# A recommender tower on one core: the pair products move to GpSimd, an accumulating DMA folds 12 fields of each tile, and the closing sum comes two tiles later

## The reference, cut to what matters

```python
x0 = prev = e                                     # (512, 32 fields, 32)
for W in (filter_0, filter_1):                    # 32*32 x 128 and 32*128 x 128
    z = einsum('bhd,bmd->bhmd', x0, prev)         # products of pairs
    cur = relu(einsum('bpd,pn->bnd', z.reshape(b, h*m, d), W))
    prev = cur
    outs.append(cur)
h = concatenate([sum over d of outs, dense_ctx])  # 128 + 128 + 16
h = relu(h @ W_top1 + b_top1); h = relu(h @ W_top2 + b_top2); y = h @ W_top3
```

## Time and profile before

| what | us |
| --- | --- |
| median of 3 runs | 1014.85 (1011.53 to 1015.65) |
| the profiled execution, its own time | 1015.16 |
| its span in the trace | 1013.4 |
| DVE busy in it | 962.2 (95%) |
| PE busy | 914.2 (90%) |
| ACT busy | 818.3 (81%) |
| POOL busy | 810.8 (80%) |

### The profile page before, as it was taken

One profiled execution on the slowest core, in us unless ns is written; L12 is line 12 of the kernel. 1 busy time (PEld: TensorE's weight loads), 2 busy tenths in 40 slices (PEclk: granted clock), 3 DMA queues, 4 the chain that ended last, 5 costly groups with the idle time before them and its releaser, 6 DMA issues.

```text
span 1013.4 us, 17901 instructions
## 1 busy us (share of the span) xinstructions
PE 914.2 (90%) x3822; PEld 713.5 (70%) x3822; DVE 962.2 (95%) x1057; ACT 818.3 (81%) x2808; POOL 810.8 (80%) x452
## 2 busy tenths in 40 slices
PE   3989899898999989899999899989899988898998
PEld 2767777777778677677776777767776766677784
DVE  4899999999999999999999999999999999999993
ACT  3878888788888878788888788878888878888892
POOL 5678889788889888889888888888888788896871
PEclk9999999899999989999999899999999999999998
DMA  5412222202222202222211222211222211222000
GB/s 190 133 51 71 71 66 70 59 23 66 71 65 69 69 18 60 70 66 68 69 39 39 70 69 65 70 42 35 71 70 64 69 37 41 70 70 64 1 1 0
DMA packets 42849, 61.18 MB, mean 60 GB/s; under 512 B 6273, under 2 KB 17153, under 8 KB 42786
## 3 DMA queue, kind: packets, MB, share of 16 engines
q1 hardware_dynamic: 38690, 58.48, 18.8%
q0 software_dynamic: 4096, 2.11, 1.4%
HBM read 56.37 MB, written 4.20 MB: 60 GB/s over the span
## 4 chain that ended last, share of the span: by engine, by line
PE 61%; DVE 20%; issue 12%; ACT 3%; POOL 2%; DMA 1%; DVEq 1%; SPq 0%; ACTq 0%; POOLq 0%
PE ps_y L621 17%; PE ps_y L627 17%; PE ps_y L622 16%; DVE csum L514 6%; DVE prod L500 6%; DVE z L474 5%; PE ps_c L608 3%; PE ps_c L609 2%; PE ps_c L610 2%; ACT prod L384 2%; DVE c_lo L479 2%; PE ps_h L632 1%; POOL prod L321 1%; PE ps_c L606 1%; POOL z_lo L310 1%
## 5 line engine op out<-in xcount | busy, mean ns | idle before, releaser
L384 ACT ACTIVATE prod<-ps_y,es 128x128 f32<-128x128 f32 x2560 | 698.8, 416 | 76.2 <-PE ps_y L627 72.6
L321 POOL TENSOR_TENSOR prod<-prod 128x1536 f32<-128x1536 f32 x129 | 450.4, 3491 | 113.6 <-DVE prod L500 96.6
L627 PE MATMUL ps_y<-w_hi,c_lo 128*128 128x512 f32 x1024 | 413.4, 404 | 49.1 <-DVE c_lo L479 49.1
L621 PE MATMUL ps_y<-w_hi,c_hi 128*128 128x512 f32 x1024 | 429.2, 419 | 28.1 <-DVE prod L500 25.0
L622 PE MATMUL ps_y<-w_lo,c_hi 128*128 128x512 f32 x1024 | 411.0, 401 | 0.0
L514 DVE TENSOR_REDUCE csum<-prod 128x64 f32<-128x1280 f32 x256 | 378.2, 1478 | 10.2 <-ACT prod L384 0.6
L474 DVE TENSOR_TENSOR z<-first,second 128x512 f32<-128x512 f32 x160 | 282.1, 1764 | 7.1 <-DMA second<-et_scratch 7.1
L627 PEld LDWEIGHTS ps_y<-w_hi,c_lo 128*128 128x128 f32 x1024 | 198.7, 194 | 105.5 <-DVE c_lo L479 62.0
L500 DVE TENSOR_TENSOR prod<-ps_y,es 128x512 f32<-128x512 f32 x384 | 256.2, 677 | 10.2 <-PE ps_y L627 10.1
L621 PEld LDWEIGHTS ps_y<-w_hi,c_hi 128*128 128x128 f32 x1024 | 198.6, 194 | 94.9 <-DVE prod L500 39.1
L310 POOL TENSOR_TENSOR z_lo<-z,z_hi 128x512 fp32r<-128x512 f32 x155 | 222.3, 1452 | 6.8 <-ACT z_hi L362 6.8
(11 more groups left out here) (59 smaller groups left out, 259.0 us busy)
## 6 DMA issues: line engine op xcount, KB each, us to landing
second<-et_scratch SPq DMA_DIRECT2D x160, 256.0 KB, 4.3
first<-et_scratch SPq DMA_DIRECT2D x32, 256.0 KB, 3.3
et_scratch<-gat SPq DMA_DIRECT2D x64, 64.0 KB
prod<-w SPq DMA_DIRECT2D x4, 512.0 KB, 7.1
gat<-table,rows_now POOLq DMA_INDIRECT x128, 2.4
wt_sb<-wt SPq DMA_DIRECT2D x2, 512.0 KB, 5.5
prod<-w0a SPq DMA_DIRECT2D x1, 320.0 KB, 3.1
prod<-w0b SPq DMA_DIRECT2D x1, 320.0 KB, 3.2
```

What stands on the lines that cost most here:

```text
L321: nc.gpsimd.tensor_tensor(high, high, low, ALU.add).then_inc(added, 1)
L384: last = nc.scalar.activation(prod[:, buffer_of(g, u), h // 2, :, h % 2], ps_y[:, bank_of(g, u, k), j * N:(j + 1) * N], ACT.Copy, scale=es ...
L621: nc.tensor.matmul(out, hi, w_hi, start=True, stop=False)
L627: nc.tensor.matmul(out, lo, w_hi, start=False, stop=True).then_inc(y_ready, 1)
```

## The change

The products of layer 0 of the groups after the first are made by GpSimd (`multiply`, L320 of the new kernel) and no longer by VectorE. GpSimd no longer adds the 12 fields itself: it issues one DMA a tile from its own queue (`fold`, L329) that reads fields 0 to 11 of the tile in `prod` (128 rows of 6,144 bytes, 786,432 bytes) and accumulates them onto fields 12 to 23 in SBUF. Like the addition it waits for banks 0 to 5 of its tile, but it stands at the end of that tile's own work, where the addition stood at the start of the next one's. VectorE's closing sum over 20 fields waits for the DMA's semaphore. Both its halves now stand in the tile two later, at k = 2 and k = 4, with the rectification at k = 6; before, the first half stood one tile later at k = 6, the second two later at k = 2. `prod` gets a fourth buffer.

Smaller parts: `c_lo` is made from `ps_c` directly (`rest_c`), ScalarE makes `c` five banks after `c_hi`, `h0` is summed in the next group, and the strided order of `ps_c` moves from the readers to the matmuls' moving operand. The last tile's addition in two pieces goes.

The diff, without some declarations:

```diff
@@ -43,15 +43,14 @@
 NK = F // HB
 RING = 6
 SLOTS = 3
-BUFS = 3
+BUFS = 4
 LASTK = KP - 1
 WARM_UP = 22
 W1_LOADS = 4
 
 ACT_BANKS = ((0, 1, 3, 5, 6),) * TG
 DVE_BANKS = tuple(tuple(k for k in range(NK) if k not in a) for a in ACT_BANKS)
-ADD = 12
-ADDS_LAST = ((0, 8), (8, 12))
+FOLD = 3 * F // 8
 HALVES = 2
 
 
...
@@ -310,15 +313,21 @@
                 nc.gpsimd.tensor_tensor(z_lo[:, k, :], z[:, k, :], z_hi[:, k, :].bitcast(F32),
                                         ALU.subtract).then_inc(z_lo_ready, 1)
 
-            def add(g, u, start=0, end=ADD):
-
-                last_bank = (2 * end - start - 1) // HB
-                lows, highs = slice(start // 2, end // 2), slice(end // 2, (2 * end - start) // 2)
+            def multiply(g, k):
+
+                pool.wait_ge(pairs_in[k], g.times(32, 32) if k == 0 else g.times(16, 16))
+                wait(pool, z_lo_ready, g.times(KP, k + 1 - KP))
+                nc.gpsimd.tensor_tensor(z[:, k, :], first[:, :], second[:, k, :], ALU.mult).then_inc(z_ready, 1)
+
+            def fold(g, u):
+
+                last_bank = 2 * FOLD // HB - 1
                 pool.wait_ge(act_scaled, signals(ACT_BANKS, g, u, last_bank))
                 pool.wait_ge(dve_scaled, signals(DVE_BANKS, g, u, last_bank))
+                pool.sem_inc(pool_passed, 1)
                 buf = buffer_of(g, u)
-                low, high = prod[:, buf, lows, :, :], prod[:, buf, highs, :, :]
-                nc.gpsimd.tensor_tensor(high, high, low, ALU.add).then_inc(added, 1)
+                pool.dma_start(prod[:, buf, FOLD // 2:FOLD, :, :], prod[:, buf, 0:FOLD // 2, :, :],
+                               accum_op=ALU.add).then_inc(folded[buf], 16)
 
             pool.wait_ge(rows_step, 5)
             for g in range(SLOTS):
...
@@ -331,17 +340,24 @@
             pool.wait_ge(first_odd_z_lo, KP // 2)
             pool.sem_inc(z_lo_ready, KP // 2)
 
+            Z_AT_FIRST = {0: ((1, 0), (1, 1), (1, 2)), 1: ((1, 3), (1, 4)), 3: ((2, 0), (2, 1))}
+            Z_LO_AT_FIRST = {1: (0, 1), 2: (2, 3, 4)}
+            Z_AT = {0: ((1, 2), (1, 3)), 1: ((1, 4),), 3: ((2, 0), (2, 1))}
+            Z_LO_AT = {0: (0, 1), 1: (2, 3), 2: (4,)}
+
             def body(g, number):
+                more = number is None or number + 1 < GROUPS
                 for u in range(TG):
-                    if not (number == 0 and u == 0):
-                        add(*before(g, u))
-                    if u < 2 and (number is None or number + 1 < GROUPS):
-                        split_z(g.plus(1), 2 * u)
-                        split_z(g.plus(1), 2 * u + 1)
-                    if u == 2 and (number is None or number + 1 < GROUPS):
-                        split_z(g.plus(1), LASTK)
+                    products = (Z_AT_FIRST if number == 0 else Z_AT).get(u, ())
+                    splits = (Z_LO_AT_FIRST if number == 0 else Z_LO_AT).get(u, ()) if more else ()
+                    for n in range(max(len(products), len(splits))):
+                        if n < len(products) and (number is None or number + products[n][0] < GROUPS):
+                            multiply(g.plus(products[n][0]), products[n][1])
+                        if n < len(splits):
+                            split_z(g.plus(1), splits[n])
                     if u >= 2 and (number is None or number + SLOTS < GROUPS):
                         gather(g.plus(SLOTS), ((0, 1), (2, 3))[u - 2])
+                    fold(g, u)
                     if number == GROUPS - 1 and u >= 2:
 
                         low, whole, high = ((wt2_lo, wt2_sb[:, :, :], wt2_hi), (wt1_lo, wt1_sb[:, 1, :], wt1_hi))[u - 2]
...
@@ -365,12 +378,21 @@
...
+
+            def rectify_hi(g):
+
+                act.wait_ge(l0_done, g.times(1, 1))
+                nc.scalar.activation(c_hi[:, g.r, :], ps_c[:, :], ACT.Relu).then_inc(c_hi_ready, 1)
+
+            def rectify_whole(g):
+
+                act.wait_ge(c_lo_ready, g.times(1, 1))
+                act.wait_ge(h0_done, g.times(1))
+                nc.scalar.activation(c[:, :], ps_c[:, :], ACT.Relu).then_inc(c_ready, 1)
 
             def scale(g, u, k):
 
...
@@ -408,7 +430,9 @@
                             if at == (u, k) and (number is None or number + n < GROUPS):
                                 split_z(g.plus(n), chunk)
                         if more and (u, k) == (3, 1):
-                            rectify(g.plus(1))
+                            rectify_hi(g.plus(1))
+                        if more and (u, k) == (3, 6):
+                            rectify_whole(g.plus(1))
 
 
             Z_HI_AT_FIRST = {(1, 0): (0, 3), (1, 1): (0, 5), (1, 2): (0, 7), (1, 3): (1, 1), (1, 4): (1, 5), (2, 0): (3, 4), (2, 1): (3, 7)}
...
@@ -476,17 +500,22 @@
...
+            def rest_c(g):
+
+                dve.wait_ge(c_hi_ready, g.times(1, 1))
+                nc.vector.scalar_tensor_tensor(out=c_lo[:, g.r, :], in0=ps_c[:, :], scalar=0.0, in1=c_hi[:, g.r, :].bitcast(F32),
+                                               op0=ALU.max, op1=ALU.subtract).then_inc(c_lo_ready, 1)
 
             def sum_h0(g):
 
+                dve.wait_ge(c_ready, g.times(1, 1))
                 nc.vector.tensor_reduce(
-                    h0[:, bass.ds(g.times(TG * BT), TG * BT)].rearrange("p (u b) -> p b u", u=TG),
-                    c[:, :].rearrange("p (b u d) -> p b u d", u=TG, b=BT), AX.X, ALU.add).then_inc(h0_done, 1)
+                    h0[:, bass.ds(g.times(TG * BT), TG * BT)], c[:, :].rearrange("p (t d) -> p t d", d=D),
+                    AX.X, ALU.add).then_inc(h0_done, 1)
 
             def scale(g, u, k):
 
...
@@ -503,15 +532,15 @@
                     es[:, g.r, u, fields].rearrange("p (a t) -> p a t", t=2).unsqueeze(2).to_broadcast([P, HB // 2, N, 2]),
                     ALU.mult).then_inc(dve_scaled, 1)
 
-            def reduce(g, u, half, start=ADD, additions=1):
+            def reduce(g, u, half):
 
                 if half == 0:
-                    dve.wait_ge(added, g.times(TG, u + additions))
+                    dve.wait_ge(folded[buffer_of(g, u)], uses_of_buffer(g, u) * 16)
                     dve.wait_ge(act_scaled, signals(ACT_BANKS, g, u, NK - 1))
                     dve.wait_ge(dve_scaled, signals(DVE_BANKS, g, u, NK - 1))
                     wait(dve, c1_ready, g.times(TG, u))
                 maps = slice(half * N // HALVES, (half + 1) * N // HALVES)
-                nc.vector.tensor_reduce(csum[:, maps], prod[:, buffer_of(g, u), start // 2:F // 2, maps, :].rearrange("p a n t -> p n a t"),
+                nc.vector.tensor_reduce(csum[:, maps], prod[:, buffer_of(g, u), FOLD // 2:F // 2, maps, :].rearrange("p a n t -> p n a t"),
                                         AX.XY, ALU.add).then_inc(reduced, 1)
 
             def rectify(g, u):
...
@@ -558,14 +584,13 @@
                         if k in DVE_BANKS[u]:
                             scale(g, u, k)
                         if k == 2 and not (number == 0 and u < 2):
+                            reduce(*before(g, u, 2), 0)
+                        if k == 4 and not (number == 0 and u < 2):
                             reduce(*before(g, u, 2), 1)
-                        if k == 4 and not (number == 0 and u < 2):
+                        if k == 6 and not (number == 0 and u < 2):
                             rectify(*before(g, u, 2))
-                        if k == 6 and not (number == 0 and u == 0):
-                            reduce(*before(g, u), 0)
-                        for (n, chunk), at in (Z_AT_FIRST if number == 0 else Z_AT).items():
-                            if at == (u, k) and (number is None or number + n < GROUPS):
-                                multiply(g.plus(n), chunk)
+                        if number != 0 and (u, k) == (0, 4):
+                            sum_h0(g)
                         if number == GROUPS - 1 and (u, k) == (1, 3):
                             round_top(wt2_hi, wt2_sb[:, :, :])
                         if number == GROUPS - 1 and (u, k) == (2, 3):
...
@@ -573,15 +598,14 @@
                         if more and (u, k) == (2, 3):
                             turn(g.plus(1))
                         if more and (u, k) == (3, 3):
-                            split_c(g.plus(1))
-                        if more and (u, k) == (3, 5):
-                            sum_h0(g.plus(1))
+                            rest_c(g.plus(1))
 
             over_groups(dve, body)
-            reduce(LAST, TG - 2, 1)
+            for half in range(HALVES):
+                reduce(LAST, TG - 2, half)
             rectify(LAST, TG - 2)
             for half in range(HALVES):
-                reduce(LAST, TG - 1, half, ADDS_LAST[-1][1], len(ADDS_LAST))
+                reduce(LAST, TG - 1, half)
             rectify(LAST, TG - 1)
             dve.wait_ge(h1_hi_ready, 2)
             nc.vector.tensor_tensor(h1_lo, ps_h1[:, :], h1_hi.bitcast(F32), ALU.subtract).then_inc(h1_lo_ready, 1)
...
@@ -602,12 +626,13 @@
```

(45 more changed lines are left out.)

## The result

The changed kernel takes 1047.08 us (median of 4 runs, 1040.32 to 1049.75); the kernel before took 1013.19 beside it. The ratio is 1.032, 95% interval 1.029 to 1.036: slower, where 910 us was forecast.

A forecast was written before the change was run, and what follows sets the result against it. VectorE was taken to bound the kernel, TensorE's floor next. A group of 26.8 for 30.31 us saves 105 us; profiled 1015.2 - 105 + 1 = 911, the median 0.3 lower: 910 us, range 878 to 972 (8 in 10).

The forecast's parts named there:

- What bounds the kernel before: Loop: VectorE full, its products stopped by GpSimd's additions; next bound TensorE's floor of 25.75 us a group.
- The fold: Adding DMA per tile: issue 1.44 us, 4.6 us on the DMA engines, landing 6.4 us after issue; fits, narrowly.
- The rival of a slow accumulating DMA: Loop: slower if a fold occupies the engines 6.3 us or lands after 11.5; 1100 us at three copies' cost; 11%.
- GpSimd: Loop: products, remainders, gathers and fold issues sum to 24.5 us a group, below TensorE's 25.75; bounds 18.7 and 30.2.
- GpSimd at 90 to 95%: Sign that the forecast holds: GpSimd's busy share in the new profile.
- The moved order of the operand: Layer 0 matmuls reading runs of 32 columns: taken as nothing, at most 2.6 us a group.
- The failed step: Loop: without two-input SBUF instructions on VectorE, GpSimd's products and `z_lo` take 1.29 us each, 12.9 us a group.
- VectorE then has 4.8 us to spare below 25.75: Loop: VectorE loses five products, 8.8 of its 29.76 us a group, and keeps 20.9.
- The sum: Group: floor 25.75 plus 1.05 for remaining waits gives 26.8 us; 105 us saved over 30 groups.
- The end: After the loop: the last fold's latency and half sums replace the addition in two pieces, 1 us later.
- The rivals: Nothing between, 880 to 893 us, 12%; GpSimd or DMA bound, 936 to 1000, 21%; no gain, 4%; slower, 11%.

The follow-up runs named there:

- e1_max: The changed kernel with the rectification of csum into c1 as a VectorE reduction by maximum over (csum, 0), in place of the plain TENSOR_SCALAR: 896.6 us, ratio 0.880.
- e9_accum: The changed kernel with the rectification's TENSOR_SCALAR in its form that also sums its output into an accumulator that nothing reads: 899.28 us, ratio 0.884.
- e10_place: The changed kernel with the plain rectification moved to right behind the bank of k = 4, the second half sum at k = 3: 940.44 us, ratio 0.924.
- e2_before_max: The kernel before the change with its rectification replaced by a reduction by maximum: 1021.25 us, ratio 1.004.
- e4_fold_only: The changed kernel with the loop's layer 0 products back on VectorE at their old places, fold by DMA and plain rectification kept: 1044.13 us, ratio 1.026.
- e6_sum_late: The changed kernel with TensorE taking the sums over d of c1 four banks later (k = 7, not 3), plain rectification kept: 1052.95 us, ratio 1.029.
- e1_again: The changed kernel with the rectification as a reduction by maximum, measured once more: 894.23 us, ratio 0.881.

## Why the prediction was wrong

Most steps held, and one that was never written down decided.

- **What bounds the kernel before** held: without the collisions a group falls from 30.31 to 26.16 us. I had 25.75 as the floor and 26.8 as the forecast.
- **The fold** held. It lands after 6.3 us in the median (6.4 forecast), and its half sum waits for nothing. Its issue takes 0.93 us, below the 1.44 taken; the next instruction starts 0.65 us behind it. GpSimd's queue takes 50.8% of the DMA engines' span, from which I estimate 4.0 us a fold once the gathers' part is off (1.4% of the span before); the 58.7% of `e1_max` give the same: near the 4.6 taken for two reads, far from a copy's 2.3. The longest fold lands after 9.8 us. The rival of a slow accumulating DMA, which begins at 11.5, is refuted.
- **GpSimd** is not the bound, as forecast: 1.23 us from one of its instructions to the next (522.40, 523.63), 1.29 taken. But its load was put too high. The sign "GpSimd at 90 to 95%" did not come, not in `e1_max` either, where it is busy 73%, or 660.2 / 32 = 20.6 us a group in place of 24.5.
- **The moved order of the operand** costs nothing: 407 ns a matmul of layer 0, as before.
- **The failed step** is "the loop of the change has no two-input SBUF instruction on VectorE, so I take 1.29 for products and `z_lo` alike", and with it "VectorE then has 4.8 us to spare below 25.75". I used the exclusion of the two engines as a rule on two-input instructions and asked only whether GpSimd would be disturbed. The rectification was never listed: one input, 128 columns, 0.21 us in the median of before, though its 28 rows of 0.7 us were there to be read. It too is shut out, and for longer than a product, through a whole run of GpSimd's. What was put at nothing came to 171.0 us in place of 41.3, and to 98.3 us of TensorE waiting for `c1`. That it was mostly short before was a matter of order: there it stood right behind the bank that GpSimd's addition waited for. The change moved it two banks on, to where GpSimd, newly loaded with runs of four, is at work. `e9_accum` shows the form, `e10_place` the place, `e2_before_max` that before the form did not matter.
- **The sum.** Taken away, the collisions give `e1_max`; 144 us lie between the two spans. TensorE's waits for `c1` are 98.3 us of them (1.0 there), and behind these stops some 165 of its matmuls run at the slow pace, about 33 us at 0.2 us each (an estimate from the distances 0.43 and 0.23). None does in the loop of `e1_max`. For a kernel without the collisions my 910 us would have been right to 2%; there the group takes 26.16 us where I had 26.8.
- **The end** was mis-sized: 1 us forecast, 12.4 measured in the changed kernel. Two rectifications are shut out there by the `z_lo` of the top network's weights (3.19 and 1.40 us), TensorE stands 1.43 and 2.78 us, and the eight float32 matmuls run at the lower clock: 16.0 in place of 8.4 us. `e1_max` still has 6.7 us: the later half sums leave a stop of 1.05 us there, and the clock falls as well.
- **The rivals** missed the mechanism as well. The one that ended slower named the DMA; none asked what GpSimd's new work would do to VectorE's remaining instructions.

That the page of the changed kernel shows no full engine is itself the sign: VectorE 80% busy and TensorE 88%, and 11% of the chain in an instruction that does 0.2 us of work.

## What to carry to other kernels

When work moves to GpSimd, list every VectorE instruction that stays, also the 0.2 us ones, and ask of each whether it is a plain form that GpSimd can shut out, as the TENSOR_SCALAR here, or one that it cannot, as the reduction and the accumulating form; then look at the longest run of GpSimd instructions without a gap, since that is what such an instruction may have to wait. A line whose maximum is 26 times its median is the place to look first. If one is found, change its form before giving up the change, and don't take the wait that TensorE reports as the cause: moving TensorE's sum later removed that wait and gained nothing.

## What the runs showed of the hardware

- A plain TENSOR_SCALAR of 128x128 float32, SBUF to SBUF, lasted 5.91 us beside a fold's issue and four GpSimd instructions in a row, and up to 12.8 us where an addition of 3.5 us stood in the run. In the changed kernel, `e4_fold_only`, `e6_sum_late` and `e10_place` every long one (38, 82, 82 and 30 of 128) ended 0.08 to 0.11 us behind a TENSOR_TENSOR of GpSimd. It was not let in between them there; in the kernel before it was, 26 times. Ten that started 0.14 to 0.20 us into a fold's issue, with a product 0.5 us behind them, took 0.23 us where others at the same distances took 5.9.
- The same operation with an accumulator took 0.273 to 0.289 us, 23 times wholly inside a GpSimd instruction. A TENSOR_REDUCE over 256 elements took 0.407 to 0.423 us, 32 times partly beside one.
- An accumulating DMA of 786,432 bytes within SBUF, 128 rows of 6,144 bytes, landed 5.6 to 9.8 us after its issue beside 1.7 MB of other loads a group, took 4.0 us of the 16 DMA engines (an estimate from their busy shares), and cost GpSimd 0.93 us.
- TensorE's granted clock was at its lower level after stops of 4.43 us (0.53 from 527.5 to 531 us of the changed kernel), and in the second half of the eight matmuls behind the stop of 1.04 us at the end of `e1_again` (0.51 from 870.5 to 878.3). It was not after every stop: behind one of 1.43 us, from 1003 to 1006 us of the changed kernel, it was 1.00. In the loop of `e1_max`, where the longest stop is 0.6 us, no matmul ran at the slow pace.
